# The routing's sigmoid from ScalarE's own table instead of silu times a reciprocal, in a macaron block of two mixture-of-experts layers around attention

## The chip, the cores and the metric

One core of one Trainium2 chip. The time is device microseconds of one execution; three executions of the kernel before are given below, and one more that was profiled.

## What is computed

A block of three residual steps on x of 2048 rows of 128 numbers, in fp32: half a mixture-of-experts layer, attention, half a mixture-of-experts layer with the same weights. The part that the change touches is the routing in the two expert layers (64 experts, 8 chosen):

```
aff = xf @ centroids.T
biased = aff + expert_biases
_, idx = jax.lax.top_k(biased, TOP_K)
sel = jnp.take_along_axis(aff, idx, axis=1)
w = jax.nn.sigmoid(sel)
w = w / (jnp.sum(w, axis=-1, keepdims=True) + 1e-08)
cw = jnp.zeros((T, E)).at[jnp.arange(T)[:, None], idx].add(w)
h = jax.nn.silu(jnp.einsum('td,edf->etf', xf, W_up))
y = jnp.einsum('etf,efd->etd', h, W_down)
routed = jnp.einsum('etd,te->td', y, cw)
```

xf is the layer-normed x. The kernel computes all 64 experts for every row and multiplies by `cw`, which is zero for those not chosen.

## The kernel before

Rows are worked in chunks of 512, four in each expert layer: n = 0 to 3 in the first, 4 to 7 in the second, with attention between them. A chunk has 33 units: unit 0 is the shared expert, units 1 to 32 are pairs of experts. Products are made of three fp32r matmuls each, from a high part (a copy to fp32r) and a low part (the rest) of both factors. The order on each engine is written out by hand, by unit; engines are tied by semaphores.

A unit passes through: `up` on TensorE (L874 to L876, into one of four PSUM buffers of `lrow`), silu on ScalarE (L399), the gate's multiply on VectorE (L588), the fp32r copy `hi_unit` on ScalarE (L410), the low part (L249, on GpSimd in two of three units, on VectorE where u is a multiple of 3), and `down` on TensorE (L914 to L916), four units after its `up` in TensorE's list. ScalarE's order is silu(u), then hi(u-1). `up(u)` waits until the buffer of unit u-4 is free, `down(u)` for the low part of u.

The routing of chunk n+1 is made inside chunk n. On TensorE the transposes stand at unit 8, the product with the centroids at unit 11 (into the PSUM bank `mp`), the transpose of the weights at unit 24. VectorE reads the product at units 12 and 13 (`pro_aff`), takes the reciprocal at unit 14 (`pro_top` step 0), the eight largest at 15, the mask of the chosen at 17 (L660 and L662), and the sum at 20. ScalarE makes the silu of `aff` at unit 15 (`pro_sil`, L418), and GpSimd multiplies silu, reciprocal and mask at unit 18 (`weights`). Since silu(a)/a is the sigmoid, the reciprocal of `aff`, kept away from zero by TINY, gives it. For n = 0 and n = 4 there is no chunk before: n = 0 is routed at the start, n = 4 inside and at the end of attention, and VectorE does the multiplications (`first_weights`, L668 and on).

In chunks 1 to 3 the second layer norm (for attention) of the chunk before is made too: GpSimd raises the variances to the power -1/2 (L330 and L331, `rstd(1, c - 1)`) at unit 14, behind the low part of unit 14; VectorE refines that at unit 16 (L611 to L613) and writes the normed rows (L615) at units 16 and 17; TensorE transposes them (L927) at unit 20. In chunk 0 ScalarE and GpSimd also split the later pieces of the expert weights, at even units up to 14.

ScalarE has its functions in tables; the instruction ACT_TABLE_LOAD changes the one in use. Copies need no change of it.

Of the kernel before, what the change touches and what calls it, by code (L numbers as in the profile page):

```python
# [23 lines left out]
P = 128  # L24
# [15 lines left out]
LOWEST = -3.4e38  # L40
TINY = 1e-15


def macaron_kernel(nc, x_d, wup_d, wdn_d, wsup_d, wsdn_d, cent_d, bias_d, wq_d, wk_d, wv_d, gates_d, out_d):
# [21 lines left out]
    with ExitStack() as ctx:  # L66
        def sb(name, shape, dt=F32, stack=ctx):
            return stack.enter_context(nc.sbuf_tensor(name, shape, dt))

        def sem(name):  # L70
            return ctx.enter_context(nc.semaphore(name))
# [46 lines left out]
        xn_a = sb("xn_a", [P, TPC, D], F32, ffn)  # L118
        biased_a, aff_a = sb("biased_a", [P, TPC, E], F32, ffn), sb("aff_a", [P, TPC, E], F32, ffn)
        gated = sb("gated", [P, NG, CH], F32, ffn)  # L120
# [5 lines left out]
        with ExitStack() as first:  # L126
# [5 lines left out]
        xnT, xn = [xnT_a, xnT_b], [xn_a, xn_b]  # L132
        biased, aff = [biased_a, biased_b], [aff_a, aff_b]
        pT = [sb("pT_hi", [P, 2, NT, GW], F32R), sb("pT_lo", [P, 2, NT, GW], F32R)]
# [38 lines left out]
        p_st, p_rs, p_xn, p_xT, p_hi, p_lo = (sem("p_" + n) for n in ("stats", "rstd", "xn", "xT", "hi", "lo"))  # L173
        p_aff, p_affs, p_bias, p_max, p_sil, p_top, p_w, p_inv, p_cw, p_cwT, p_cwr = (
            sem("p_" + n) for n in ("aff", "aff_read", "biased", "max", "sil", "top", "w", "inv", "cw", "cwT", "cwT_read"))

# [140 lines left out]
        def _(pool):  # L317
            steps = [0]

            def link(ins):  # L320

                steps[0] += 1
                ins.then_inc(s_pool, 1)
                pool.wait_ge(s_pool, steps[0])
# [12 lines left out]
            def weights(n):  # L337

                pool.wait_ge(p_sil, n + 1)
                pool.wait_ge(p_top, n + 1)  # L340
                link(nc.gpsimd.tensor_tensor(rec[:, :, :], rec[:, :, :], sil[:, :, :], ALU.mult))
                nc.gpsimd.tensor_tensor(rec[:, :, :], rec[:, :, :], rest[:, :, :], ALU.mult).then_inc(p_w, 1)

# [45 lines left out]
        def _(act):  # L389
# [26 lines left out]
            def pro_sil(n):  # L416
                act.wait_ge(p_affs, n + 1)
                nc.scalar.activation(sil[:, :, :], aff[n // NCH][:, :, :], ACT.Silu).then_inc(p_sil, 1)  # L418

# [54 lines left out]
            for f in range(2):  # L474
                for c in range(NCH):
# [14 lines left out]
                    for u in range(UNITS):  # L490
# [74 lines left out]
        def _(dve):  # L565
            steps = [0]

            def link(ins):

                steps[0] += 1  # L570
                ins.then_inc(s_dve, 1)
                dve.wait_ge(s_dve, steps[0])
# [60 lines left out]

            def pro_aff(n, step):

                f = n // NCH
                ps = mp[:, 0:TPC * E].rearrange("p (t e) -> p t e", e=E)
                if step == 0:
                    dve.wait_ge(p_aff, n + 1)
                    link(nc.vector.tensor_scalar(rec[:, :, :], ps, 0.0, 2 * TINY, ALU.is_ge, ALU.mult))  # L640
                    nc.vector.scalar_tensor_tensor(out=aff[f][:, :, :], in0=ps, scalar=TINY, in1=rec[:, :, :],
                                                   op0=ALU.subtract, op1=ALU.add).then_inc(p_affs, 1)
                else:
                    nc.vector.tensor_tensor(biased[f][:, :, :], ps, bc(bias[:, :]), ALU.add).then_inc(p_bias, 1)

            def pro_top(n, step):

                b = biased[n // NCH]
                if step == 0:
                    dve.wait_ge(p_affs, n + 1)  # L650
                    nc.vector.reciprocal(rec[:, :, :], aff[n // NCH][:, :, :])
                if step == 1:
# [11 lines left out]
            def first_weights(n):  # L664

                dve.wait_ge(p_sil, n + 1)
                dve.wait_ge(p_top, n + 1)
                link(nc.vector.tensor_tensor(rec[:, :, :], rec[:, :, :], sil[:, :, :], ALU.mult))  # L668
                nc.vector.tensor_tensor(rec[:, :, :], rec[:, :, :], rest[:, :, :], ALU.mult).then_inc(p_w, 1)
                pro_sum(n)  # L670
# [54 lines left out]
            for f in range(2):  # L725
                for c in range(NCH):
                    n = f * NCH + c
                    if c == 0:
                        if f == 0:
# [6 lines left out]
                            pro_lo(n)  # L736
                            pro_aff(n, 0)
                            pro_aff(n, 1)
                            for step in range(3):
                                pro_top(n, step)  # L740
                            first_weights(n)
                    for u in range(UNITS):
# [5 lines left out]
                        if c + 1 < NCH:  # L748
# [55 lines left out]
                if f == 0:  # L804
# [28 lines left out]
                    for t in range(NT):  # L833
# [20 lines left out]
                        if t == T_AFF:  # L854
                            pro_aff(NCH, 0)
                            pro_aff(NCH, 1)
                        if t > T_AFF:
                            pro_top(NCH, t - T_AFF - 1)
                    for j in range(KB):
# [287 lines left out]
```

## Time and profile before

| | us |
|---|---|
| three runs | 581.55, 583.32, 583.37 |
| median | 583.32 |
| profiled execution | 583.93 |
| its span | 582.1 |

In the profile, PE is TensorE's matmuls, PEld its weight loads, DVE VectorE, ACT ScalarE, POOL GpSimd and SP SyncE. L418 is line 418 of the kernel printed above. A matmul's own duration overlaps with its neighbours, so the starts are what to read on TensorE. On the other engines too, neighbours overlap by up to about 0.1 us.

### The profile page before, as it was taken

The numbers are of one execution on the slowest core, as the hardware profiler recorded it, in microseconds if no ns is written. First come the engines' busy times: TensorE is split into PE (matmuls) and PEld (weight loads), VectorE is DVE, ScalarE is ACT, GpSimd is POOL, SyncE is SP. The second block draws the span as 40 slices with busy tenths as digits, with TensorE's granted clock in tenths as the row PEclk, the third lists the DMA queues.
The fourth block names the chain that finished last, engine by engine and source line by source line (L and its number), as shares of the span: only waits on it lengthen the run. The fifth ranks groups of instructions, "written<-read, shape, count | busy, mean of one in ns | idle before, by whom it ended". The sixth has DMA issues, their size and how long they took to land.

```text
span 582.1 us, 8666 instructions
## 1 busy us (share of the span) xinstructions
PE 546.1 (94%) x2715; PEld 441.7 (76%) x2715; DVE 437.9 (75%) x913; ACT 406.2 (70%) x800; POOL 280.7 (48%) x248
## 2 busy tenths in 40 slices
PE   3489999899989999989999999899999999999996
PEld 2368777687867777669999999768777777877884
DVE  3778769977996686577777988788768968875663
ACT  4558776686768777476666666677776787687774
POOL 4478765666576567300000000055664766566563
PEclk9689999999999999999999999999999999999999
DMA  6465564455536645000000000046664555666562
GB/s 187 135 199 179 172 193 144 131 176 181 161 125 188 178 155 162 1 1 1 2 0 2 1 2 1 1 139 185 182 193 152 161 198 142 178 175 196 180 191 82
DMA packets 47837, 73.25 MB, mean 126 GB/s; under 512 B 8944, under 2 KB 13488, under 8 KB 47792
## 3 DMA queue, kind: packets, MB, share of 16 engines
q1 hardware_dynamic: 47792, 72.71, 41.0%
q8 instruction: 21, 0.34, 0.2%
q14 instruction: 24, 0.20, 0.1%
HBM read 70.58 MB, written 2.10 MB: 125 GB/s over the span
## 4 chain that ended last, share of the span: by engine, by line
PE 76%; DVE 12%; ACT 3%; POOL 3%; issue 3%; DMA 2%; SPq 1%; POOLq 0%; DVEq 0%; ACTq 0%
PE lrow L874 11%; PE lrow L875 11%; PE lrow L876 11%; PE bank L914 9%; PE bank L916 8%; PE bank L915 8%; PE bank L920 6%; PE bank L1069 3%; PE bank L1071 3%; PE bank L1070 3%; DVE rs L613 2%; DVE gated L588 2%; POOL gpart_lo L249 2%; DVE rs L611 1%; PE bank L875 1%
## 5 line engine op out<-in xcount | busy, mean ns | idle before, releaser
L249 POOL TENSOR_TENSOR gpart_lo<-gated,gpart_hi 128x512 fp32r<-128x512 f32 x176 | 226.6, 1293 | 192.5 <-ACT gpart_hi L410 188.4
L399 ACT ACTIVATE lrow<-lrow 128x512 f32<-128x512 f32 (+1 forms) x256 | 149.7, 585 | 62.0 <-PE lrow L876 61.7
L588 DVE TENSOR_TENSOR gated<-lrow,wide 128x512 f32<-128x512 f32 x170 | 116.5, 685 | 48.4 <-ACT lrow L399 43.7
L410 ACT CAST gpart_hi<-gated 128x512 fp32r<-128x512 f32 x176 | 107.9, 613 | 8.0 <-DVE gated L588 7.3
L914 PE MATMUL bank<-gpart_lo,wdn_hi 128*128 128x512 f32 x256 | 102.2, 399 | 1.6 <-POOL gpart_lo L249 1.4
L916 PE MATMUL bank<-gpart_hi,wdn_hi 128*128 128x512 f32 x256 | 101.6, 397 | 0.0
L915 PE MATMUL bank<-gpart_hi,wdn_lo 128*128 128x512 f32 x256 | 101.1, 395 | 0.0
L588 DVE TENSOR_TENSOR lrow<-lrow,wide 128x512 f32<-128x512 f32 x78 | 54.0, 693 | 30.8 <-ACT lrow L399 30.8
L410 ACT CAST gpart_hi<-lrow 128x512 fp32r<-128x512 f32 (+1 forms) x88 | 52.0, 591 | 30.8 <-DVE lrow L588 30.7
L810 DVE TENSOR_TENSOR pT_lo<-bank,pT_hi 128x512 fp32r<-128x512 f32 x64 | 43.6, 683 | 25.8 <-ACT pT_hi L532 25.8
L249 DVE TENSOR_TENSOR gpart_lo<-lrow,gpart_hi 128x512 fp32r<-128x512 f32 (+1 forms) x88 | 59.9, 680 | 1.3 <-ACT gpart_hi L410 0.6
L914 PEld LDWEIGHTS bank<-gpart_lo,wdn_hi 128*128 128x128 f32 x256 | 48.2, 188 | 16.0 <-POOL gpart_lo L249 4.2
L916 PEld LDWEIGHTS bank<-gpart_hi,wdn_hi 128*128 128x128 f32 x256 | 48.2, 188 | 11.8
L525 ACT ACTIVATE prow<-lrow,nmax 128x512 f32<-128x512 f32 x64 | 44.4, 696 | 17.8 <-DVE nmax L719 17.8
L915 PEld LDWEIGHTS bank<-gpart_hi,wdn_lo 128*128 128x128 f32 x256 | 48.2, 188 | 11.1
L532 ACT CAST pT_hi<-bank 128x512 fp32r<-128x512 f32 x64 | 38.0, 593 | 25.2 <-PE bank L920 25.0
L874 PE MATMUL lrow<-xnT_lo_a,wup_hi 128*128 128x512 f32 x128 | 53.5, 418 | 0.4 <-DVE gpart_lo L249 0.4
L874 PE MATMUL lrow<-xnT_lo_b,wup_hi 128*128 128x512 f32 x128 | 52.0, 406 | 0.0
L875 PE MATMUL lrow<-xnT_hi_a,wup_lo 128*128 128x512 f32 x128 | 51.7, 404 | 0.0
L876 PE MATMUL lrow<-xnT_hi_a,wup_hi 128*128 128x512 f32 x128 | 51.7, 404 | 0.0
L875 PE MATMUL lrow<-xnT_hi_b,wup_lo 128*128 128x512 f32 x128 | 50.7, 396 | 0.0
L876 PE MATMUL lrow<-xnT_hi_b,wup_hi 128*128 128x512 f32 x128 | 50.2, 392 | 0.0
(181 smaller groups left out, 989.6 us busy)
## 6 DMA issues: line engine op xcount, KB each, us to landing
wide<-gates_dram SPq DMA_DIRECT2D x496, 128.0 KB, 3.0
raw<-in_w_up SPq DMA_DIRECT2D x8, 256.0 KB, 3.9
raw<-in_w_down SPq DMA_DIRECT2D x8, 256.0 KB, 4.2
x<-in_x SPq DMA_DIRECT2D x4, 256.0 KB, 4.3
gates_dram<-gates SPq DMA_DIRECT2D x8, 128.0 KB, 2.3
out_dram<-x SPq DMA_DIRECT2D x4, 256.0 KB, 3.2
raws<-in_wv SPq DMA_DIRECT2D x1, 64.0 KB, 2.2
raws<-in_wq SPq DMA_DIRECT2D x1, 64.0 KB, 2.1
```

The costliest lines, as they stand in the source:

```text
L249: return eng.tensor_tensor(gpart[1][0:m, U % NGP, :], gated_at(U)[0:m, :], gpart[0][0:m, U % NGP, :].bitcast(F32), ALU.subtract)
L399: nc.scalar.activation(dst[0:m, :], hid[U % NH][0:m, :], ACT.Silu).then_inc(s_silu, 1)
L410: nc.scalar.copy(gpart[0][0:m, U % NGP, :], gated_at(U)[0:m, :]).then_inc(s_ghi, 1)
L525: nc.scalar.activation(prow[:, j * CH:(j + 1) * CH], lrow[:, j * CH:(j + 1) * CH], ACT.Exp, bias=nmax[:, t % 2:t % 2 + 1], accum_out=psums ...
L588: nc.vector.tensor_tensor(gated_at(U), a, b, ALU.mult).then_inc(s_gated, 1)
L810: nc.vector.tensor_tensor(pT[1][at], tb[q % 2][:, :].rearrange("p (k n) -> p k n", n=P), pT[0][at].bitcast(F32), ALU.subtract).then_inc(a_ ...
L874: nc.tensor.matmul(out, a[0], b[1], start=True, stop=False)
L875: nc.tensor.matmul(out, a[1], b[0], start=False, stop=False)
L876: return nc.tensor.matmul(out, a[0], b[0], start=False, stop=True)
L914: nc.tensor.matmul(y, w[0], g[1], start=(u == 0), stop=False)
L915: nc.tensor.matmul(y, w[1], g[0], start=False, stop=False)
L916: nc.tensor.matmul(y, w[0], g[0], start=False, stop=(u == UNITS - 1)).then_inc(s_down, 1)
```

## The change

ScalarE computes the sigmoid directly, from PSUM, at unit 13; the silu of the units uses another table, so there is one load before the sigmoid and one before the next silu. VectorE's comparison, shift and reciprocal go, and one of the two multiplications of `weights` and `first_weights`. The read of the product and the biased scores stand together at unit 12. For n = 4, whose bank is needed by attention, VectorE copies the product to `aff_b` and the sigmoid reads that, at the place that `pro_sil` had.

```diff
-                link(nc.gpsimd.tensor_tensor(rec[:, :, :], rec[:, :, :], sil[:, :, :], ALU.mult))
-                nc.gpsimd.tensor_tensor(rec[:, :, :], rec[:, :, :], rest[:, :, :], ALU.mult).then_inc(p_w, 1)
+                nc.gpsimd.tensor_tensor(rec[:, :, :], sil[:, :, :], rest[:, :, :], ALU.mult).then_inc(p_w, 1)
...
             def pro_sil(n):
-                act.wait_ge(p_affs, n + 1)
-                nc.scalar.activation(sil[:, :, :], aff[n // NCH][:, :, :], ACT.Silu).then_inc(p_sil, 1)
+                act.wait_ge(p_bias, n + 1)
+                src = flat(aff_b) if n == NCH else mp[:, 0:TPC * E]
+                nc.scalar.activation(flat(sil), src, ACT.Sigmoid).then_inc(p_sil, 1)
...
-                            if u == 15:
+                            if u == 13:
                                 pro_sil(n + 1)
...
-            def pro_aff(n, step):
+            def pro_aff(n):
 
                 f = n // NCH
                 ps = mp[:, 0:TPC * E].rearrange("p (t e) -> p t e", e=E)
-                if step == 0:
-                    dve.wait_ge(p_aff, n + 1)
-                    link(nc.vector.tensor_scalar(rec[:, :, :], ps, 0.0, 2 * TINY, ALU.is_ge, ALU.mult))
-                    nc.vector.scalar_tensor_tensor(out=aff[f][:, :, :], in0=ps, scalar=TINY, in1=rec[:, :, :],
-                                                   op0=ALU.subtract, op1=ALU.add).then_inc(p_affs, 1)
-                else:
-                    nc.vector.tensor_tensor(biased[f][:, :, :], ps, bc(bias[:, :]), ALU.add).then_inc(p_bias, 1)
+                dve.wait_ge(p_aff, n + 1)
+                if n == NCH:
+                    nc.vector.tensor_copy(aff_b[:, :, :], ps)
+                nc.vector.tensor_tensor(biased[f][:, :, :], ps, bc(bias[:, :]), ALU.add).then_inc(p_bias, 1)
...
-                if step == 0:
-                    dve.wait_ge(p_affs, n + 1)
-                    nc.vector.reciprocal(rec[:, :, :], aff[n // NCH][:, :, :])
...
-                link(nc.vector.tensor_tensor(rec[:, :, :], rec[:, :, :], sil[:, :, :], ALU.mult))
-                nc.vector.tensor_tensor(rec[:, :, :], rec[:, :, :], rest[:, :, :], ALU.mult).then_inc(p_w, 1)
+                nc.vector.tensor_tensor(rec[:, :, :], sil[:, :, :], rest[:, :, :], ALU.mult).then_inc(p_w, 1)
...
                             if u == 12:
-                                pro_aff(n + 1, 0)
-                            if u == 13:
-                                pro_aff(n + 1, 1)
-                            if u == 14:
-                                pro_top(n + 1, 0)
+                                pro_aff(n + 1)
```

## Rows read from the trace of the kernel before

**Rows 1.** The page: span, TensorE's line, the chain that ended last by engine.
```profile
span 582.1 us, 8666 instructions
...
PE 546.1 (94%) x2715; PEld 441.7 (76%) x2715; DVE 437.9 (75%) x913; ACT 406.2 (70%) x800; POOL 280.7 (48%) x248
...
PE 76%; DVE 12%; ACT 3%; POOL 3%; issue 3%; DMA 2%; SPq 1%; POOLq 0%; DVEq 0%; ACTq 0%
```

**Rows 2.** Windows: n = 5; length, busy of each engine, clock, DMA.
```profile
428.00:478.00 50.00, 49.51 (x223) 39.17 (x223) 40.31 (x80) 37.65 (x70) 31.58 (x27) 1.00 0.54 171
```

**Rows 3.** Groups by line, whole span; busy us, mean ns, idle before.
```profile
L651 DVE RECIPROCAL rec<-aff_a 128x256 f32<-128x256 f32 x4 | 7.0, 1741 | 0.0
...
L640 DVE TENSOR_SCALAR rec<-bank 128x256 f32<-128x256 f32 x8 | 3.3, 414 | 2.9 <-PE bank L876 2.9
...
L418 ACT ACT_TABLE_LOAD x2 | 2.6, 1283 | 0.0
...
L641 DVE SCALAR_TENSOR_TENSOR aff_a<-bank,rec 128x256 f32<-128x256 f32 x4 | 1.7, 424 | 0.1
...
L418 ACT ACTIVATE sil<-aff_a 128x256 f32<-128x256 f32 x4 | 1.7, 418 | 0.0
```

**Rows 4.** Timeline of ScalarE at the start; start us, us, what.
```profile
16.39 0.62 ACT L462 CAST wdn_hi<-raw 128x512 fp32r<-128x512 f32 x1 [1.81 <-DMA raw<-in_w_down]
17.02 1.28 ACT L418 ACT_TABLE_LOAD   x1
18.32 0.42 ACT L418 ACTIVATE sil<-aff_a 128x256 f32<-128x256 f32 x1
```

**Rows 5.** Timeline, all engines, n = 5, units 12 to 17.
```profile
448.94 0.60 ACT L410 CAST gpart_hi<-lrow 128x512 fp32r<-128x512 f32 x1
...
449.84 0.58 ACT L399 ACTIVATE lrow<-lrow 128x512 f32<-128x512 f32 x1 [0.31 <-PE lrow L876]
...
450.34 0.61 ACT L410 CAST gpart_hi<-gated 128x512 fp32r<-128x512 f32 x1
...
451.03 2.69 POOL L249 TENSOR_TENSOR gpart_lo<-gated,gpart_hi 128x512 fp32r<-128x512 f32 x2 [1.50 <-ACT gpart_hi L410]
...
452.85 0.67 DVE L588 TENSOR_TENSOR lrow<-lrow,wide 128x512 f32<-128x512 f32 x1
...
453.83 0.40 PE L914 MATMUL bank<-gpart_lo,wdn_hi 128*128 128x512 f32 x1
```

**Rows 6.** Timeline, all engines, n = 0, units 13 to 17.
```profile
51.07 0.59 ACT L410 CAST gpart_hi<-lrow 128x512 fp32r<-128x512 f32 x1
...
51.83 0.58 ACT L399 ACTIVATE lrow<-lrow 128x512 f32<-128x512 f32 x1 [0.17 <-PE lrow L876]
...
53.53 2.56 POOL L249 TENSOR_TENSOR gpart_lo<-gated,gpart_hi 128x512 fp32r<-128x512 f32 x2 [0.24 <-ACT gpart_hi L410]
...
55.83 0.40 PE L914 MATMUL bank<-gpart_lo,wdn_hi 128*128 128x512 f32 x1
```

**Rows 7.** Timeline, all engines, n = 1, units 15 to 20.
```profile
104.76 1.30 POOL L249 TENSOR_TENSOR gpart_lo<-gated,gpart_hi 128x512 fp32r<-128x512 f32 x1
...
106.34 1.04 POOL L331 TENSOR_TENSOR rs<-rs,mhalf 128x4 f32<-128x4 f32 x1
...
107.47 0.15 DVE L611 TENSOR_TENSOR rs<-rs 128x4 f32<-128x4 f32 x1
...
112.82 0.33 PE L927 MATMUL bank<-ident,xn 128*128 128x128 f32 x1 [1.36 <-DVE xn L615]
```

**Rows 8.** Timeline, all engines, the weights of n = 0 on VectorE.
```profile
19.32 1.45 POOL L335 TENSOR_TENSOR wup_lo<-raw,wup_hi 128x512 fp32r<-128x512 f32 x1 [0.97 <-ACT wup_hi L462]
...
20.14 0.66 DVE L680 TENSOR_SCALAR wsum<-wsum 128x4 f32<-128x4 f32 x1
```

**Rows 9.** Timeline of ScalarE, the start of n = 4.
```profile
375.97 0.37 ACT L539 CAST oT_hi<-bank 128x256 fp32r<-128x256 f32 x1 [3.33 <-PE bank L876]
...
378.89 0.59 ACT L423 CAST cwT<-bank 128x512 fp32r<-128x512 f32 x1 [0.98 <-PE bank L920]
```

More of the change, by code:

```diff
@@ L40 @@
 LOWEST = -3.4e38
-TINY = 1e-15
 def macaron_kernel(nc, x_d, wup_d, wdn_d, wsup_d, wsdn_d, cent_d, bias_d, wq_d, wk_d, wv_d, gates_d, out_d):
@@ L118, in macaron_kernel @@
         xn_a = sb("xn_a", [P, TPC, D], F32, ffn)
-        biased_a, aff_a = sb("biased_a", [P, TPC, E], F32, ffn), sb("aff_a", [P, TPC, E], F32, ffn)
+        biased_a, _ = sb("biased_a", [P, TPC, E], F32, ffn), sb("free_a", [P, TPC, E], F32, ffn)
         gated = sb("gated", [P, NG, CH], F32, ffn)
@@ L132, in macaron_kernel @@
         xnT, xn = [xnT_a, xnT_b], [xn_a, xn_b]
-        biased, aff = [biased_a, biased_b], [aff_a, aff_b]
+        biased = [biased_a, biased_b]
         pT = [sb("pT_hi", [P, 2, NT, GW], F32R), sb("pT_lo", [P, 2, NT, GW], F32R)]
@@ L173, in macaron_kernel @@
         p_st, p_rs, p_xn, p_xT, p_hi, p_lo = (sem("p_" + n) for n in ("stats", "rstd", "xn", "xT", "hi", "lo"))
-        p_aff, p_affs, p_bias, p_max, p_sil, p_top, p_w, p_inv, p_cw, p_cwT, p_cwr = (
-            sem("p_" + n) for n in ("aff", "aff_read", "biased", "max", "sil", "top", "w", "inv", "cw", "cwT", "cwT_read"))
+        p_aff, p_bias, p_max, p_sil, p_top, p_w, p_inv, p_cw, p_cwT, p_cwr = (
+            sem("p_" + n) for n in ("aff", "biased", "max", "sil", "top", "w", "inv", "cw", "cwT", "cwT_read"))
         e_y, e_yT, e_x, e_st, e_rs, e_xn, e_xT, e_hi, e_lo = (
@@ L736, in _ @@
                             pro_lo(n)
-                            pro_aff(n, 0)
-                            pro_aff(n, 1)
-                            for step in range(3):
+                            pro_aff(n)
+                            for step in range(1, 3):
                                 pro_top(n, step)
@@ L854, in _ @@
                         if t == T_AFF:
[L855 to L858, printed above, removed]
+                            pro_aff(NCH)
+                        if t == T_AFF + 2:
+                            pro_top(NCH, 1)
                     for j in range(KB):
```

## The prediction

> **What bounds the kernel now.** I read the page first: TensorE is busy for 94% of the span and carries 76% of the chain that ended last; VectorE carries 12% of it, ScalarE only 3% [rows 1]. The reader should see a kernel whose length is that of TensorE's list plus the gaps in it. The table of windows shows how few gaps there are: in the sixth chunk (n = 5) TensorE is busy 49.51 us of 50.00, at the full granted clock [rows 2]. So what delays a TensorE matmul there is paid in full, and nothing is given back later. The question of this change is therefore how late the other engines may be before a `down` matmul waits for them.
>
> The timeline of n = 5 gives that margin [rows 5]. The fp32r copy of unit 13 (`hi_unit`) starts on ScalarE at 450.34; GpSimd then makes the low parts of units 13 and 14, a pair that starts at 451.03 and takes 2.69 us, so the first, at the 1.30 us of one [rows 7], is done at 452.33; `down(13)` starts on TensorE at 453.83. The margin is 1.50 us. ScalarE has little to catch up with: in this stretch it idles 0.31 us a unit [rows 5], waiting for TensorE. In n = 0 the weight pieces are split by ScalarE in the same loop and margins are smaller: low part 13 starts at 53.53, is done 1.28 us (half of the pair's 2.56) later at 54.81, and `down(13)` starts at 55.83, a margin of 1.02 us [rows 6].
>
> **The change, part by part.**
>
> *Removed from VectorE*, eight times: the comparison (0.41 us), the shift by TINY (0.42 us) and the reciprocal (1.74 us), 2.57 us of instructions [rows 3] and about 2.45 us of its queue, since neighbours overlap a little. GpSimd and, for n = 0 and 4, VectorE lose one 128x256 multiply. For n = 4 a copy of 0.41 us (priced as the comparison, which has its shape) comes in for the two removed ones, beside attention, where nothing waits for it: 0.
>
> *Added to ScalarE*: two table loads for each sigmoid, one ahead of it, one ahead of the next silu. All loads in the trace take 1283 ns [rows 3]. What surrounds one is seen at n = 0: the copy ends at 17.01, the load runs from 17.02 to 18.30, the activation starts at 18.32 [rows 4]. A switch costs the queue 1.30 us. The sigmoid itself reads PSUM instead of SBUF; I price it as the silu, 0.42 us [rows 3].
>
> The Trainium skill (ScalarE: Activation LUTs, section "What ACT_TABLE_LOAD costs") gives 2.66 us a switch, 1.28 of load and 1.38 of drain; rows 4 agree with the first figure and show no drain. With its figure the sum below would be 6 x 2 x 1.36 = 16 us larger, an estimate from that page. I take the row.
>
> *Moved*: `pro_sil` goes from unit 15 to unit 13 on ScalarE, behind `hi_unit(12)`. Behind it in the queue stand silu(14), hi(13), silu(15), hi(14) and so on: everything on which `down(13)` and later ones depend. It now waits for `p_bias`, which VectorE gives after gate(12), before hi(12) is over; no further wait.
>
> *The burst.* 2 x 1.30 + 0.42 = 3.02 us lies between hi(12) and silu(14). In n = 5 hi(12) ends at 448.94 + 0.60 = 449.54, so silu(14) starts at 452.56, where it started at 449.84: 2.72 us late [rows 5]. hi(13) is late by the same 2.72, low part 13 too, and `down(13)` by 2.72 - 1.50, 1.2 us, and the start after a wait: 1.3 us.
>
> *Does VectorE's relief repay this?* Before, gate(15) started at 452.85, late because of the reciprocal [rows 5]. Now hi(13) follows silu(14) by 0.50 (as before) and silu(15) follows that by 0.50: 453.56; it takes 0.58, and gate(15) starts at 454.17, 1.32 us later than before. VectorE idles through the burst; its 2.45 us saved are spent waiting for ScalarE. From gate(15) on its list (maximum, gates, match) is full and everything keeps this lateness. So both routes give 1.3 us, and n = 4, 5 and 6, whose chunks have the same spacing, cost 3 x 1.3 = **3.9 us**.
>
> *n = 0.* hi(12) ends at 51.66; silu(14) goes from 51.83 to 54.68, 2.85 late; `down(13)` is late by 2.85 - 1.02, with the start after a wait **1.9 us** [rows 6].
>
> *n = 1 and 2.* The same burst, and a third party. In these chunks GpSimd's queue has, behind low part 14, the power for the second layer norm (`rstd(1, ..)`), on which VectorE's L611 waits at unit 16. Before, low part 14 ended at 106.06, the power at 107.38, and L611 started at 107.47, just as VectorE came free [rows 7]: no margin. Now low parts 13 and 14 start 2.7 us late, but run without the gap between them, 2.56 instead of 2.69 us [rows 5, 6], so the power ends 2.55 us late. L611, the normalised rows and the transposes at unit 20, where TensorE already waited for VectorE in this chunk (1.36 us before one of them) [rows 7], are all 2.5 us late. VectorE alone would be 1.3 late; GpSimd's queue doubles it. 2 x 2.5 = **5.0 us**. Should L611 now also collide with low part 16, as L613 may do anyway, 1.3 us are added in each; that is the upper bound, 2.6 more.
>
> *n = 3 and 7* have no routing for a next chunk: 0. *Start of the first half:* the sigmoid waits for a weight piece and a load as the silu did. One 128x256 multiply fewer is on VectorE's way (0.42 us, as L641 of that shape), but L680 (4 numbers a partition) took 0.66 us and ended when GpSimd's instruction from 19.32 to 20.77 did [rows 8]. Started that much earlier it would end at the same 20.8. I take 0, with -0.5 as the bound; the second load falls in ScalarE's wait for the gate weights. The Trainium skill (SBUF — State Buffer, on the shared port pair) says that the loser of the two engines blocks for a whole instruction. This row agrees: by that page 0, without it -0.5.
>
> *Start of the second half (n = 4):* one load replaces the silu's, one is new, at about 376.34, after the last copy of attention's output. It ends at 377.62; the two silus behind it, at a pitch of 0.5, end by 378.7, before the copy to `cwT` behind them, which waited until 378.89 for TensorE [rows 9]. Hidden: 0; if that cover were gone, 1.3 us.
>
> *Sum:* 1.9 + 5.0 + 3.9 = 10.8 us. The profiled execution took 583.93 us (582.1 of span, 1.8 around it); 583.93 + 10.8 = 594.7. It stands 0.6 above the median of 583.32, so against that: **594.1 us**, 1.9% slower.
>
> **The rivals.**
>
> *A. GpSimd's queue does not double the cost in n = 1 and 2.* If the power gets done in time, they cost 1.3 each by TensorE's and VectorE's routes: 594.1 - 2.4 = 591.7. For it: before, VectorE stood in no wait there. Against: low part 14 is ahead of the power in one queue, and must itself follow the burst. 0.12.
>
> *B. Faster: the burst is not seen.* If the two functions share a table, or the loads are slipped into ScalarE's idle moments, ScalarE's queue is as long as before, and VectorE's 2.45 us a chunk count: TensorE's waits for normalised rows in n = 1 and 2 (1.36 us at one of them, and a smaller one) vanish, some 1.9 a chunk, and the start gives up to 0.5: 583.3 - 3.8 - 0.5 = 579.0. It decides if the burst stays below about 1.5 us, the margin of rows 5. Against: no row shows a load beside another ScalarE instruction, and a chunk offers 0.3 us of idle at a time. The case that the change does not do what it says (no loads) is this one. 0.06.
>
> *C. A switch costs much more inside a full queue than in rows 4.* With margins used up all of it passes: at twice the row, 6 x 2 x 1.3 = 15.6 more, 609.7. The trace's loads stand behind copies or after waits, never in the middle of silus; but the one of rows 4 had a full queue on both sides. The Trainium skill's figure, named above, is on this side. 0.04.
>
> *D. Nothing to measure.* The margins would have to be twice as large; the slacks of rows 5 and 6 exclude it, unless gains of B and losses cancel. 0.03.
>
> **How the numbers follow.** The forecast has 0.75, A 0.12, B 0.06, C 0.04, D 0.03. The prediction is 594.1. The bounds: from below A, -0.5 at the start and about 1 for small margins misread over six chunks, 590; from above 2.6 for the collision and 1.3 for the second half's start, 598. The range is 589.5 to 598.5; it holds the forecast and A. Differences of 0.3% are about what a measurement of this kernel tells from none. Slower 0.91, same 0.03, faster 0.06.
>
> **What would show it.** In the changed profile: 1283 ns loads, 16 for the sigmoids and their returns, with the three others; silu(14) some 3.0 us after the end of hi(12) in every routing chunk; VectorE idle there, before gate(14), with ScalarE as releaser; a new wait of TensorE on GpSimd's low part at `down(13)` of about 1.2 us; L611 waiting about 1 us for L331's result in n = 1 and 2 alone; chunk lengths up by 1.9, 2.5, 2.5, 0, 1.3, 1.3, 1.3, 0. The prediction is wrong if the loads overlap with other ScalarE work, if a chunk after the burst wins back part of it (a gap of TensorE elsewhere that closes), or if low part 14 does not hold up the power.

## The result, and the profile after

| | before | after |
|---|---|---|
| median, us | 582.62 (4 runs, 581.55 to 583.37) | 595.01 (4 runs, 593.92 to 597.45) |
| profiled execution, us | 583.93 | 595.85 |
| its span, us | 582.1 | 594.0 |

The changed kernel takes 1.0194 times as long (95% interval 1.0168 to 1.022). The medians differ by 12.4 us, and their quotient, 1.021, lies inside the interval too. The two profiled executions differ by 11.92 us, and that is the difference taken apart below.

Line numbers of the changed kernel: silu L397, `hi_unit` L408, the sigmoid L417, the gate L587, low part L248, `up` L860 to L862, `down` L900 to L902, the power L330, its refinement L610 to L612, the normed rows L614, their transposes L913, mask L653 and L655.

The page after, which answers to [rows 1]: span, engines, and the chain that ended last.

```profile
span 594.0 us, 8649 instructions
...
PE 549.5 (92%) x2715; PEld 443.8 (75%) x2715; DVE 416.6 (70%) x888; ACT 423.9 (71%) x814; POOL 276.6 (47%) x242
...
PE 71%; DVE 10%; ACT 6%; POOL 5%; issue 4%; DMA 2%; SPq 1%; POOLq 0%; DVEq 0%; ACTq 0%
```

VectorE has 21 us less to do and the kernel is 12 us longer. ScalarE has 18 us more: 20.6 us of loads for the sigmoids, where 2.6 stood before. In the chain that ended last, ScalarE's share has doubled from 3 to 6% and GpSimd's has risen from 3 to 5%. The groups by line say which instructions (busy us, mean ns, idle before):

```profile
L900 PE MATMUL bank<-gpart_lo,wdn_hi 128*128 128x512 f32 x256 | 103.5, 404 | 8.6 <-POOL gpart_lo L248 8.4
...
L417 ACT ACT_TABLE_LOAD x8 | 10.3, 1283 | 0.1
L397 ACT ACT_TABLE_LOAD x8 | 10.3, 1283 | 0.1
...
L469 ACT ACT_TABLE_LOAD x1 | 1.3, 1283 | 0.7 <-PEq L1126 0.7
L436 ACT ACT_TABLE_LOAD x1 | 1.3, 1283 | 0.0
L439 ACT ACT_TABLE_LOAD x1 | 1.3, 1283 | 0.0
```

Sixteen loads and three others, all of 1283 ns. TensorE's matmuls on a low part (L900) had 8.4 us of waits for GpSimd ahead of them.

How late the changed kernel is at a point, against the trace of before, can be read off TensorE's first `up` of each chunk. The same rows of the two kernels, first before (chunks 5 and 6), then after:

```profile
425.95 0.39 PE L874 MATMUL lrow<-xnT_lo_b,small_hi 128*64 128x512 f32 x1
...
476.08 0.40 PE L874 MATMUL lrow<-xnT_lo_b,small_hi 128*64 128x512 f32 x1
```

```profile
435.61 0.39 PE L860 MATMUL lrow<-xnT_lo_b,small_hi 128*64 128x512 f32 x1
...
486.88 0.39 PE L860 MATMUL lrow<-xnT_lo_b,small_hi 128*64 128x512 f32 x1
```

Chunk 5 took 50.13 us and takes 51.27: 1.14 more. The whole table, made in this way, in us; everything up to `up(11)` of n = 0 is counted as the start:

| | start | n=0 | n=1 | n=2 | n=3 | n=4 | n=5 | n=6 | n=7 | sum |
|---|---|---|---|---|---|---|---|---|---|---|
| predicted | 0 | 1.9 | 2.5 | 2.5 | 0 | 1.3 | 1.3 | 1.3 | 0 | 10.8 |
| measured | -0.54 | 1.76 | 4.66 | 2.54 | 0.01 | 1.23 | 1.14 | 1.12 | 0.01 | 11.93 |

Within a chunk the lateness comes in steps. In n = 4, 5 and 6 the only large step up is at unit 18 of TensorE's list (1.32, 1.31 and 1.32), just ahead of which `down(13)` stands; 0.17 to 0.18 is given back at units 22 and 23. The same is given back there in experiment 1, so it belongs to VectorE's shorter list.

### The profile page after: what moved, and what is told of

Read it like the earlier page. It is cut to its first block, busy times and chain, and to the rows that moved or that the text cites. A ratio compares the mean times of both kernels' runs of the same rounds, so it can differ in the third digit from the quotient of the medians.

```text
span 594.0 us, 8649 instructions
## 1 busy us (share of the span) xinstructions
PE 549.5 (92%) x2715; PEld 443.8 (75%) x2715; DVE 416.6 (70%) x888; ACT 423.9 (71%) x814; POOL 276.6 (47%) x242
## 4 chain that ended last, share of the span: by engine, by line
PE 71%; DVE 10%; ACT 6%; POOL 5%; issue 4%; DMA 2%; SPq 1%; POOLq 0%; DVEq 0%; ACTq 0%
PE lrow L860 11%; PE lrow L861 10%; PE lrow L862 10%; PE bank L900 8%; PE bank L902 8%; PE bank L901 7%; PE bank L906 5%; POOL gpart_lo L248 3%; PE bank L1055 3%; PE bank L1057 3%; PE bank L1056 3%; ACT gpart_hi L408 2%; DVE rs L610 2%; DVE rs L612 1%; ACT lrow L397 1%
## 5 line engine op out<-in xcount | busy, mean ns | idle before, releaser
L248 POOL TENSOR_TENSOR gpart_lo<-gated,gpart_hi 128x512 fp32r<-128x512 f32 x176 | 227.2, 1296 | 211.4 <-ACT gpart_hi L408 207.3
L397 ACT ACTIVATE lrow<-lrow 128x512 f32<-128x512 f32 (+1 forms) x256 | 149.6, 584 | 66.4 <-PE lrow L862 65.4
L587 DVE TENSOR_TENSOR gated<-lrow,wide 128x512 f32<-128x512 f32 x170 | 117.0, 688 | 71.3 <-ACT lrow L397 64.5
L408 ACT CAST gpart_hi<-gated 128x512 fp32r<-128x512 f32 x176 | 107.8, 613 | 10.2 <-DVE gated L587 9.8
L900 PE MATMUL bank<-gpart_lo,wdn_hi 128*128 128x512 f32 x256 | 103.5, 404 | 8.6 <-POOL gpart_lo L248 8.4
L902 PE MATMUL bank<-gpart_hi,wdn_hi 128*128 128x512 f32 x256 | 102.1, 399 | 0.0
L587 DVE TENSOR_TENSOR lrow<-lrow,wide 128x512 f32<-128x512 f32 x78 | 54.3, 696 | 35.7 <-ACT lrow L397 35.7
L408 ACT CAST gpart_hi<-lrow 128x512 fp32r<-128x512 f32 (+1 forms) x88 | 52.0, 591 | 22.3 <-DVE lrow L587 22.1
L900 PEld LDWEIGHTS bank<-gpart_lo,wdn_hi 128*128 128x128 f32 x256 | 48.6, 190 | 25.4 <-POOL gpart_lo L248 11.6
L248 DVE TENSOR_TENSOR gpart_lo<-lrow,gpart_hi 128x512 fp32r<-128x512 f32 (+1 forms) x88 | 60.0, 682 | 1.1 <-ACT gpart_hi L408 0.6
L902 PEld LDWEIGHTS bank<-gpart_hi,wdn_hi 128*128 128x128 f32 x256 | 48.6, 190 | 12.0
L860 PE MATMUL lrow<-xnT_lo_a,wup_hi 128*128 128x512 f32 x128 | 53.9, 421 | 0.2 <-DVE gpart_lo L248 0.2
L862 PE MATMUL lrow<-xnT_hi_a,wup_hi 128*128 128x512 f32 x128 | 52.1, 407 | 0.0
L860 PE MATMUL lrow<-xnT_lo_b,wup_hi 128*128 128x512 f32 x128 | 51.7, 404 | 0.0
L862 PE MATMUL lrow<-xnT_hi_b,wup_hi 128*128 128x512 f32 x128 | 50.2, 392 | 0.0
```

The source lines that it names most:

```text
L248: return eng.tensor_tensor(gpart[1][0:m, U % NGP, :], gated_at(U)[0:m, :], gpart[0][0:m, U % NGP, :].bitcast(F32), ALU.subtract)
L397: nc.scalar.activation(dst[0:m, :], hid[U % NH][0:m, :], ACT.Silu).then_inc(s_silu, 1)
L408: nc.scalar.copy(gpart[0][0:m, U % NGP, :], gated_at(U)[0:m, :]).then_inc(s_ghi, 1)
L587: nc.vector.tensor_tensor(gated_at(U), a, b, ALU.mult).then_inc(s_gated, 1)
L860: nc.tensor.matmul(out, a[0], b[1], start=True, stop=False)
L862: return nc.tensor.matmul(out, a[0], b[0], start=False, stop=True)
```

## The burst, read in n = 5

The burst is the load, the sigmoid and the load back, one behind the other in ScalarE's queue. The timeline of the changed kernel (start us, us, what, idle before and who ended it); it answers to [rows 5].

```profile
458.60 0.59 ACT L408 CAST gpart_hi<-lrow 128x512 fp32r<-128x512 f32 x1
...
459.21 1.28 ACT L417 ACT_TABLE_LOAD   x1
...
460.51 0.38 ACT L417 ACTIVATE sil<-bank 128x256 f32<-128x256 f32 x1
...
460.91 1.28 ACT L397 ACT_TABLE_LOAD   x1
...
462.20 0.58 ACT L397 ACTIVATE lrow<-lrow 128x512 f32<-128x512 f32 x1
...
462.82 0.69 DVE L587 TENSOR_TENSOR gated<-lrow,wide 128x512 f32<-128x512 f32 x1 [2.81 <-ACT lrow L397]
...
463.39 2.51 POOL L248 TENSOR_TENSOR gpart_lo<-gated,gpart_hi 128x512 fp32r<-128x512 f32 x2 [4.20 <-ACT gpart_hi L408]
...
464.70 0.49 PE L900 MATMUL bank<-gpart_lo,wdn_hi 128*128 128x512 f32 x1 [1.05 <-POOL gpart_lo L248]
```

The copy ends at 459.19 and the next silu starts at 462.20: 3.01 us for two loads and a sigmoid, nothing else between them. VectorE idles 2.81 us ahead of gate(14) and GpSimd 4.20 us ahead of its pair; the first low part of the pair is done at 464.65 (half of 2.51 after 463.39), and `down(13)` starts at 464.70 after a wait.

## n = 1: where the miss is

```profile
107.33 2.52 POOL L248 TENSOR_TENSOR gpart_lo<-gated,gpart_hi 128x512 fp32r<-128x512 f32 x2 [4.21 <-ACT gpart_hi L408]
...
110.12 1.04 POOL L330 TENSOR_TENSOR rs<-rs,mhalf 128x4 f32<-128x4 f32 x1
...
111.13 1.30 POOL L248 TENSOR_TENSOR gpart_lo<-gated,gpart_hi 128x512 fp32r<-128x512 f32 x1
111.19 1.25 DVE L610 TENSOR_TENSOR rs<-rs 128x4 f32<-128x4 f32 x1 [1.03 <-POOL rs L330]
...
116.27 1.03 DVE L614 TENSOR_SCALAR xn<-x,mv,rs 128x128 f32<-128x128 f32 x2
...
116.66 0.47 PE L913 MATMUL bank<-ident,xn 128*128 128x128 f32 x1 [2.63 <-DVE xn L614]
```

These rows answer to [rows 7]. The power follows the two low parts and is done at 111.16; VectorE waited 1.03 us for it and then needed 1.25 us for four numbers a partition (it took 0.15 before), while GpSimd's low part runs beside it. The transposes wait 2.63 us, 1.27 more than before: with the step of 1.30 at unit 18 that is 2.6. The long L610 is no addition: before, GpSimd's low part of unit 16 lay beside the last of the three instructions of the refinement, and that one took 1.15 us; now it takes 0.16. Rows of before, then of after:

```profile
107.68 1.29 POOL L249 TENSOR_TENSOR gpart_lo<-gated,gpart_hi 128x512 fp32r<-128x512 f32 x1 [0.31 <-ACT gpart_hi L410]
...
107.85 1.15 DVE L613 SCALAR_TENSOR_TENSOR rs<-rs 128x4 f32<-128x4 f32 x1
```

```profile
112.68 0.16 DVE L612 SCALAR_TENSOR_TENSOR rs<-rs 128x4 f32<-128x4 f32 x1
```

In n = 2 it is the same to the hundredth (a wait of 2.63 at 175.14), and that chunk costs 2.54.

Only n = 1 has a further 1.9 us (steps of 0.84 and 1.06 at units 22 and 23). The windows around it (from and to; length; busy of PE, PEld, DVE, ACT, POOL; granted clock; DMA), before and after:

```profile
116.00:120.00 4.00, 4.00 (x20) 3.15 (x19) 3.93 (x9) 3.34 (x8) 3.19 (x4) 1.00 0.59 186
```

```profile
112.00:116.00 4.00, 2.03 (x10) 1.40 (x8) 3.86 (x15) 1.10 (x2) 1.62 (x2) 1.00 0.18 66
116.00:120.00 4.00, 3.12 (x8) 2.35 (x9) 3.94 (x8) 2.06 (x5) 3.08 (x5) 0.51 0.19 69
120.00:124.00 4.00, 4.00 (x12) 3.11 (x12) 3.54 (x7) 2.39 (x6) 2.71 (x3) 0.63 0.61 210
...
176.00:180.00 4.00, 3.77 (x17) 2.75 (x17) 3.87 (x8) 3.58 (x7) 3.65 (x4) 1.00 0.38 113
```

TensorE is busy from 120 to 124 and has 12 matmuls in those 4 us, where the kernel before has 21: its granted clock is at the lower level (0.5, 1.2 GHz) from 116.12 to 122.94. It had been busy 2.03 of the 4 us ahead of 116. In n = 2 there is the same wait, and TensorE was busy for only 1.00 of the 4 us from 172 to 176, yet the clock stayed full (last row).

## The experiments

Each was timed beside the kernel before on the same chip: 1 to 4 on one chip and 5 to 8 on another (585.0 us for the kernel before on both), 9 and the repeat of 8 on a third (585.2). The row `after` is from the first comparison, where the kernel before had 582.62. So rows are compared by their ratios and not by their medians. The columns n=1 to end give how late TensorE starts the chunk, against the one trace of before, in us; they are of one profiled execution each.

| kernel | median | ratio (interval) | n=1 | n=2 | n=3 | n=4 | n=5 | n=6 | n=7 | end |
|---|---|---|---|---|---|---|---|---|---|---|
| after | 595.01 | 1.0194 (1.0168 to 1.022) | 1.22 | 5.88 | 8.42 | 8.43 | 9.66 | 10.80 | 11.92 | 11.93 |
| 1 silu twice, no loads | 583.46 | 0.9979 (0.9964 to 0.9995) | -1.83 | -1.70 | -1.65 | -1.63 | -1.92 | -2.09 | -2.28 | -2.28 |
| 2 before + loads | 599.45 | 1.0253 (1.0232 to 1.0274) | 2.05 | 5.69 | 8.03 | 8.05 | 10.52 | 12.90 | 15.24 | 15.25 |
| 3 power at 12 | 591.21 | 1.0119 (1.0077 to 1.0161) | 3.14 | 4.59 | 5.97 | 5.29 | 6.46 | 7.61 | 8.73 | 8.74 |
| 4 sigmoid at 17 | 587.21 | 1.0046 (1.0027 to 1.0064) | 1.02 | 0.58 | 0.13 | 0.16 | 1.30 | 2.47 | 3.61 | 3.62 |
| 5 sigmoid at 15 | 593.20 | 1.0144 (1.0113 to 1.0175) | 0.20 | 3.16 | 6.39 | 6.39 | 7.85 | 9.13 | 10.44 | 10.45 |
| 6 before, power at 12 | 584.29 | 0.9985 (0.9967 to 1.0003) | 0.05 | 0.07 | 1.10 | 0.42 | 0.45 | 0.47 | 0.43 | 0.44 |
| 7 tanh | 582.79 | 0.9958 (0.9942 to 0.9974) | -1.88 | -1.94 | -2.08 | -1.88 | -2.19 | -2.35 | -2.58 | -2.57 |
| 8 tanh, power at 12 | 579.86 | 0.9916 (0.9895 to 0.9937) | -1.10 | -1.88 | -2.70 | -3.37 | -3.57 | -3.73 | -3.92 | -3.91 |
| 8 again | 579.20 | 0.9901 (0.9881 to 0.9921) | -3.30 | -4.03 | -4.83 | -5.49 | -5.66 | -5.83 | -6.02 | -6.02 |
| 9 and norm earlier | 581.71 | 0.9945 (0.9926 to 0.9965) | -1.25 | -1.49 | -1.84 | -1.15 | -1.26 | -1.42 | -1.61 | -1.60 |

**1. The change without its loads.** The sigmoid's place takes a silu, whose table is the one in use; the routing weights of the output are then others, the work is the same.

```diff
-                nc.scalar.activation(flat(sil), src, ACT.Sigmoid).then_inc(p_sil, 1)
+                nc.scalar.activation(flat(sil), src, ACT.Silu).then_inc(p_sil, 1)
```

> The changed kernel with the silu function in the sigmoid's place, so that no table is changed inside a chunk; the routing weights are other numbers, everything else stands where it stood. If the two loads are the cost: the burst between hi(12) and silu(14) falls from 3.0 to 0.4 us, no down matmul waits, and the time is that of the kernel before or a little less, 580.5 to 582.5 us. I expect no gain from VectorE's saved 2.45 us a chunk in n = 1 and 2, since L610 (the refinement of the layer norm) then waits for GpSimd's power, which ends where it ended before. If instead the new place of the sigmoid, its read from PSUM or the shorter VectorE list is the cost: 590 or more. If VectorE's saved time is worth what rival B says: 579.

583.46 us, ratio 0.9979. All of the loss is the loads; what VectorE was relieved of is worth 0.2 to 0.3 us in each of n = 4 to 6 and nothing in n = 1 and 2. There VectorE comes to the refinement earlier than before and waits 0.52 us for GpSimd's power, as was expected.

**2. The loads without the change.** The kernel before, with one sigmoid of one number a partition at unit 13.

```diff
+                            if u == 13:
+                                nc.scalar.activation(eps[:, 4:5], eps[:, 0:1], ACT.Sigmoid)
```

> The kernel before, with a sigmoid of one number per partition put into ScalarE's list at unit 13 of the six routing chunks: it brings two table loads and about 0.2 us, and takes nothing off VectorE. My theory: silu(14) is 2.5 us late, and VectorE, which still has its reciprocal, stands 2.3 us later at gate(15); about 2.3 us in each of n = 0, 4, 5, 6 and 2.5 in n = 1, 2: 14 us, with a longer stretch of half clock in n = 1 up to 16, so 596 to 599. VectorE's relief in the change is then worth only some 4 us of the 15 us that it frees. If the relief were worth all it frees, the loads alone would cost 12.4 + 6 x 2.45 = 27 us: 609.

599.45 us, a ratio of 1.0253 where the whole change has 1.0194. Here VectorE still has its reciprocal, right behind the loads, and n = 4 to 6 cost 2.3 to 2.5 each:

```profile
464.08 1.75 DVE L653 RECIPROCAL rec<-aff_b 128x256 f32<-128x256 f32 x1
...
465.37 0.49 PE L916 MATMUL bank<-gpart_lo,wdn_hi 128*128 128x512 f32 x1 [0.87 <-POOL gpart_lo L249]
...
468.16 0.50 PE L876 MATMUL lrow<-xnT_lo_b,wup_hi 128*128 128x512 f32 x1 [0.43 <-DVE gpart_lo L249]
```

After `down(13)`, TensorE waits twice more, for VectorE's low parts of units 15 and 18 (0.43 us here, 0.48 at `up(22)`). So what the change takes away is worth about 1.2 us a chunk once ScalarE is late, though it was worth 0.2 in experiment 1. That the reciprocal and its two helpers are all of these 1.2 is argued: this kernel also keeps the silu of `aff` on ScalarE at unit 15 (0.42 us) and GpSimd's second multiply, and its mask (named below at experiment 4) took 1.55 us in n = 5 where the changed kernel has 0.42, while its burst is 0.2 us shorter. n = 1 costs 1.3 more than n = 2 (3.64 and 2.34); the granted clock was at the lower level from 119.20 to 122.62.

**3. GpSimd's power ahead of the late low parts.** The changed kernel with `rstd(1, c - 1)` at unit 12 on GpSimd.

```diff
-                        if f == 0 and c and u == 14:
+                        if f == 0 and c and u == 12:
```

> The changed kernel with the power of the second layer norm (rstd(1, ..)) at unit 12 of GpSimd's list, ahead of low parts 13 and 14. If GpSimd's queue doubles the cost in n = 1 and 2: L610 no longer waits for it, VectorE is 1.3 us late there instead of 2.5, and the time falls by 2.5 us; if the stretch of half clock at 116 to 123 us comes from TensorE's longer wait at unit 20, it goes too, 2 us more: 590.5 to 592.5. If VectorE's own list sets that wait: no change, 595.

591.21 us. The rows of n = 1 to set beside those above:

```profile
105.31 1.04 POOL L330 TENSOR_TENSOR rs<-rs,mhalf 128x4 f32<-128x4 f32 x1
...
109.24 2.52 POOL L248 TENSOR_TENSOR gpart_lo<-gated,gpart_hi 128x512 fp32r<-128x512 f32 x2 [2.89 <-ACT gpart_hi L408]
...
112.00 0.15 DVE L610 TENSOR_TENSOR rs<-rs 128x4 f32<-128x4 f32 x1
...
117.41 0.33 PE L913 MATMUL bank<-ident,xn 128*128 128x128 f32 x1 [1.46 <-DVE xn L614]
```

VectorE waits for nothing at L610, which takes 0.15 us, and the transposes wait 1.46 where they waited 2.63. n = 1 and 2 have one large step each, 1.31 at unit 18: the doubling was GpSimd's queue. The stretch at the lower clock in n = 1 is not in this trace, but there is one in n = 0, from 58.96 to 62.37, behind the wait for low part 13 (1.78 us; it was 1.77 in the changed kernel, where the clock stayed full); it cost 1.5. One trace each does not show that the edit removed the stretch in n = 1.

**4 and 5. The same burst at another unit.**

```diff
-                            if u == 13:
+                            if u == 17:
```

> The changed kernel with the sigmoid and its two loads at unit 17 of ScalarE's list instead of unit 13. In n = 1 and 2 ScalarE there idles 1.9 us for gate(17) before, so the burst is mostly hidden, and VectorE's mask no longer collides with low part 17: -0.9 us each. In n = 4, 5, 6 hi(17) stands behind the burst, and its margin is 1.5 as at unit 13: +1.25 each; n = 0: +1.3. With -0.5 at the start: 582.6 + 2.8, so 584 to 587. If a switch costs its full 3 us wherever it stands: 595 or more.

587.21 us. n = 4 to 6 cost 1.14 to 1.17 each, as much as with the burst at unit 13 (1.12 to 1.23). The step up, 1.26, is at unit 22 now, and `down(17)` waits for GpSimd's low part:

```profile
460.63 1.27 POOL L248 TENSOR_TENSOR gpart_lo<-gated,gpart_hi 128x512 fp32r<-128x512 f32 x1 [2.82 <-ACT gpart_hi L408]
...
461.95 0.50 PE L900 MATMUL bank<-gpart_lo,wdn_hi 128*128 128x512 f32 x1 [1.07 <-POOL gpart_lo L248]
```

But n = 1 and 2 gain 0.45 each; 0.9 was expected. The burst stands behind the power and falls into the time in which TensorE stood in its wait for the normed rows anyway, so that no further wait shows. The gain comes with VectorE's mask (L662 before), which stands ahead of the second pair of normed rows. In n = 1 and 2 of every other run it lies beside a low part of GpSimd and takes 1.46 to 1.55 us; here the burst holds GpSimd's low part of unit 17 back until 112.69, and the mask is over by then. A row of before, then of this run:

```profile
111.05 1.47 DVE L662 TENSOR_TENSOR rest<-rest,biased_a 128x256 f32<-128x256 f32 x1
```

```profile
112.13 0.43 DVE L655 TENSOR_TENSOR rest<-rest,biased_a 128x256 f32<-128x256 f32 x1
```

With `u == 15` in the same line:

> The changed kernel with the sigmoid and its loads back at unit 15, where the silu of the kernel before stood: does the move from 15 to 13 cost anything by itself? By the same reckoning the burst now lies between hi(14) and silu(16): gate(16) and low(15) are 2.0 us late on VectorE, up(19) and up(22) wait for them, in every routing chunk; GpSimd's power is in front of the burst and no longer late. n = 0, 1, 2, 4, 5, 6 cost some 2.0 each, 12, less 0.8 at the start: 11 us more than before, ratio 1.018 to 1.022, with a longer stretch of half clock up to 1.024. If the move to 13 is what costs: ratio 1.010 or less.

593.20 us, a ratio of 1.0144 where 1.018 to 1.022 was expected. n = 4 to 6 cost 1.3 to 1.5, less than the 2.0 of the expectation. The first to be late is `up(19)`, as expected: low part 15 is VectorE's, done in place in `lrow`, and `up(19)` waits for that buffer.

```profile
465.16 0.50 PE L860 MATMUL lrow<-xnT_lo_b,wup_hi 128*128 128x512 f32 x1 [1.22 <-DVE gpart_lo L248]
```

n = 1 and 2 cost 2.96 and 3.23. Of each, 1.5 is there by `up(20)`, and 0.7 is a longer wait for the normed rows (2.07 and 2.06 us, where the kernel before has 1.36 and 1.38). The rest, 0.8 and 1.0, falls in stretches at the lower clock, 3.4 us each (from 115.25 and 173.28).

**6. The power at unit 12 in the kernel before.** The edit of experiment 3.

> The kernel before with the power at unit 12 of GpSimd's list instead of 14. VectorE came to the refinement (L611) 0.09 us after the power was done, so it waited for its own list, not for GpSimd: no change, ratio 0.998 to 1.002. If GpSimd's power was already what held TensorE's transposes at unit 20: up to 3.5 us faster, 0.994.

584.29 us, ratio 0.9985, an interval that includes 1. n = 1 takes as long as before to 0.02 us: GpSimd's queue did not hold VectorE there in the kernel before. In n = 3 it did. No routing is made there, so VectorE comes early, and at 212.62 of the kernel before L611 had waited 0.59 us for the power; here it waits for nothing, and the chunk is 0.7 us shorter. One stretch at the lower clock (from 167.84) cost 1.1 in n = 2, behind a wait for the normed rows (1.37) that the kernel before has in the same place (1.38).

**7. Half of tanh instead of the sigmoid.** sigmoid(a) = (1 + tanh(a/2)) / 2, and the half cancels against the sum, with 2e-8 for 1e-8. GpSimd adds the 1 beside other work, for the chunks routed inside others; VectorE does both in one instruction for n = 0 and 4.

```diff
+                link(nc.gpsimd.tensor_scalar(rec[:, :, :], sil[:, :, :], 1.0, None, ALU.add))
...
-                nc.gpsimd.tensor_tensor(rec[:, :, :], sil[:, :, :], rest[:, :, :], ALU.mult).then_inc(p_w, 1)
+                nc.gpsimd.tensor_tensor(rec[:, :, :], rec[:, :, :], rest[:, :, :], ALU.mult).then_inc(p_w, 1)
...
-                nc.scalar.activation(flat(sil), src, ACT.Sigmoid).then_inc(p_sil, 1)
+                nc.scalar.activation(flat(sil), src, ACT.Tanh, scale=0.5).then_inc(p_sil, 1)
```

> The changed kernel with tanh(x/2) for the sigmoid: sigmoid is (1 + tanh(x/2))/2, the half cancels in the normalisation (with 2e-8 for 1e-8 beside the sum), and the 1 is added by GpSimd ahead of its multiply (in VectorE's multiply for n = 0 and 4). If tanh stands in the table that silu is taken from, the trace has 5 loads and the time is that of the run with silu in the sigmoid's place, 1 to 2.5 us below the kernel before, ratio 0.996 to 0.999. If it needs a table of its own, the time is that of the changed kernel.

582.79 us, ratio 0.9958. In this table and in experiment 1's, what lies ahead of n = 1 is mostly the start, of which more below. All loads of its trace:

```profile
L398 ACT ACT_TABLE_LOAD x2 | 2.6, 1283 | 0.0
L470 ACT ACT_TABLE_LOAD x1 | 1.3, 1283 | 0.7 <-PEq L1128 0.7
L437 ACT ACT_TABLE_LOAD x1 | 1.3, 1283 | 0.0
L440 ACT ACT_TABLE_LOAD x1 | 1.3, 1283 | 0.0
```

Five, as many as before: in the chunks, tanh stands beside silu without a load. It needs none behind the exponential of attention either: the tanh of n = 4 runs at 368.14 with no load ahead of it, and the load stands ahead of the next silu. With the loads gone the kernel runs as experiment 1 did: from the start of n = 1 on it wins 0.7, and experiment 1 won 0.45.

**8. Tanh, and the power at unit 12.**

> The same with the power at unit 12 of GpSimd's list. Now nothing stands between VectorE's saved 2.45 us and the normed rows of n = 1 and 2: TensorE's waits at unit 20 (1.9 us in each) go. 3.8 us less than the tanh kernel, ratio 0.988 to 0.992. If the saved time has no use even then, because something else is late for unit 20: as the tanh kernel.

579.86 us, ratio 0.9916. The gain in n = 1 and 2 is 0.8 each where up to 1.9 was expected, and 0.7 in n = 3, which was not expected; experiments 3 and 6, which have the same edit, have it too. As a second look:

> The version with tanh and GpSimd's power at unit 12 once more, beside the one with the norm earlier on the same chip, so that the two are compared directly. Expected: ratio to before 0.991 to 0.992, as in its first run.

579.20 us, ratio 0.9901, a little below the 0.991 to 0.992 expected. What TensorE still waits for at unit 20 in n = 1 of this run, and what VectorE did ahead of it:

```profile
103.53 0.15 DVE L611 TENSOR_TENSOR rs<-rs 128x4 f32<-128x4 f32 x1
...
104.12 1.58 DVE L615 TENSOR_SCALAR xn<-x,mv,rs 128x128 f32<-128x128 f32 x2
...
107.11 1.49 DVE L656 TENSOR_TENSOR rest<-rest,biased_a 128x256 f32<-128x256 f32 x1
108.53 0.88 DVE L615 TENSOR_SCALAR xn<-x,mv,rs 128x128 f32<-128x128 f32 x2
...
108.99 0.79 PE L915 MATMUL bank<-ident,xn 128*128 128x128 f32 x2 [0.80 <-DVE xn L615]
```

The mask (L656) takes 1.49 us here, beside a low part of GpSimd from 107.03 to 108.32; in experiment 4, clear of it, the same instruction took 0.43. The second pair of rows stands behind it.

**9. The norm two units earlier on VectorE as well.**

```diff
-                                if u == 16:
+                                if u == 14:
...
-                                if u == 17:
+                                if u == 15:
```

> The version with tanh and GpSimd's power issued at unit 12, and VectorE's n=1 norm refinement and multiply issued two units earlier, at units 14 and 15 instead of 16 and 17. Theory: what TensorE still waits for at the transposes of unit 20 in n=1 and n=2 (0.8 us each twice) is VectorE's late rows, so the wait goes: up to 1.3 us in each of the two chunks, 2.6 us below the version without this edit, ratio to before 0.985 to 0.989. Rival: the rows are late because VectorE's four numbers collide with GpSimd's low parts wherever they are put, or because the VectorE queue as a whole is the later one; then no change, ratio 0.991 to 0.992. Second rival: at units 14 and 15 the refinement waits for GpSimd's power and holds back the gate behind it; then up to 2 us slower in the two chunks.

581.71 us, ratio 0.9945, where 0.985 to 0.989 was expected: slower than experiment 8 beside it on the chip (0.9901, the intervals don't meet). The wait at unit 20 is gone (the step there is -2.17 against the kernel before), and two others have come, 0.39 us ahead of `down(19)` for a low part of GpSimd, and a larger one at `up(19)`:

```profile
102.20 1.27 DVE L611 TENSOR_TENSOR rs<-rs 128x4 f32<-128x4 f32 x1
...
103.70 1.17 DVE L613 SCALAR_TENSOR_TENSOR rs<-rs 128x4 f32<-128x4 f32 x1
...
105.42 0.69 DVE L588 TENSOR_TENSOR lrow<-lrow,wide 128x512 f32<-128x512 f32 x1
...
108.37 0.50 PE L862 MATMUL lrow<-xnT_lo_a,wup_hi 128*128 128x512 f32 x1 [1.14 <-DVE gpart_lo L248]
```

The refinement now stands beside the pair of low parts 13 and 14 on GpSimd and takes 1.27 and 1.17 us in two instructions of 0.15 to 0.17. gate(15) starts at 105.42, behind it and the first rows. In the repeat of experiment 8 it starts at 100.93, in a chunk that began 2.05 us earlier, so it is 2.4 us later now. `up(19)` waits for unit 15's buffer. This step is 1.16 to 1.30 in each of n = 1, 2 and 3. Against the repeat, n = 1 and 2 cost some 0.5 more each and n = 3 costs 1.3 more: experiment 8 wins 0.7 in it, and here it loses 0.7.

So the expectation was wrong, and neither rival was right as a whole. The first named the collision with GpSimd's low parts, which the rows show, but said that nothing would change. The second said slower, but named a wait for GpSimd's power, which the rows do not show, and did not count n = 3. Experiment 8 is the best version: 5 to 6 us faster than the kernel before.

## Why the prediction was right

594.1 us was predicted and 595.01 measured, inside the range of 589.5 to 598.5, and slower, as forecast at 0.91. The mechanism is the one that was forecast, and the terms of the chunks came out within 0.2 us but for n = 1. That the sum is as near as it is, 10.8 against 11.92, is in part luck: 1.9 us more in n = 1 and 0.5 less at the start, neither of them in the sum, partly cancel. By its steps:

- **Removed from VectorE, nothing gained.** Right for n = 1 to 6: experiment 1 has all of that relief and no loads, and wins 0.2 to 0.3 us a chunk in n = 4 to 6 and none in n = 1 and 2. The words that VectorE's 2.45 us "are spent waiting for ScalarE" say too much: by experiment 2, without the relief n = 4 to 6 would have cost some 2.4 us each, so about half of it held the cost down to the 1.3 of the sum.
- **A switch costs 1.30 us of queue.** Right: 459.21 to 460.51 and 460.91 to 462.20. The sixteen loads of the sigmoids and their returns all take 1.31 us from the end of the instruction before to the start of the next, and twelve of them stand in the middle of the silus of a chunk. Case C is excluded, and the runs decide against the 2.66 us that the Trainium skill gives (ScalarE: Activation LUTs, section "What ACT_TABLE_LOAD costs"): its 1.28 of load agrees, its 1.38 of drain does not show.
- **The burst, 3.0 us, and the margin of 1.50 us.** Right: 3.01, and a step of 1.32 against 1.3. What is given back later (0.17 to 0.18) was not in the sum, and "nothing is given back later" was wrong by that much.
- **n = 0, 1.9.** 1.76 measured from `up(11)` on: a step of 2.0 at unit 18, and the rest given back.
- **GpSimd doubles it in n = 1 and 2, 2.5 each.** Right: 2.54 in n = 2, and experiment 3 takes the power out of the late queue and leaves 1.31. Case A is excluded. Experiment 6 shows that in n = 1 and 2 this was no wait of the kernel before: the change made it. "In n = 1 and 2 alone" was wrong: in n = 3, L610 waits 0.59 us for the power in both kernels, at no added cost. The collision of L610 with low part 16, given as a possible 1.3 more in each, did happen (1.25 us), but it only took the place of that of L613 in the kernel before, so nothing was added.
- **Start, 0 with -0.5 as the bound.** -0.54 in the profiled pair, but that it lies at the bound is luck. The multiply is gone, and as predicted L672 (L680 before) still ended only when GpSimd's instruction beside it did (19.53 and 19.50), after 0.93 us. In this execution a weight piece also landed 1.05 us earlier (its copy starts at 15.34, at 16.39 in [rows 4]), and the multiply by the inverse sum started 1.27 us earlier, of which that piece is most. The rest is the clock's. The kernel before had the lower level from 20.10 to 30.34; in the changed one matmuls are at the slow pitch (0.43 us) only until 27.07, and it is 2.05 us ahead at `down(0)`. Then it has the lower level from 37.61 to 44.44 where the kernel before had it from 40.58 to 43.99, and 1.5 us are given back by `up(11)`. The start differs from run to run: of two executions of the same kernel, experiment 8 and its repeat, the one that had no stretch at the lower clock from 37.8 to 44.6 started chunk 1 2.2 us ahead of the other. No gain or loss of the start below that can be told from these traces.
- **n = 4's start, 0.** Right: n = 4 is entered as late as n = 3 was (8.42 and 8.43).
- **The burst is not seen (case B), or only noise (D).** Excluded by the sixteen loads and by experiment 1 against the change.
- **What was missing: 1.9 us of TensorE's clock in n = 1.** The text priced waits as waits alone. Behind a wait of 2.63 us the granted clock fell to its lower level for 6.8 us. The wait alone does not decide it: n = 2 of the same execution had the same wait and none of it. Two of the three other executions of the changed kernel had spans of 592.1 and 592.4 against 594.0, the third 595.6; they have no trace of their own, and their mean granted clocks (0.994, 0.985 and 0.984, against 0.988) do not single it out, so that the difference is this stretch is not shown. What decides whether the clock falls stays open.

Of the expectations of the experiments, that of experiment 9 failed, and three failed in size. Experiment 8 gained 0.8 of 1.9 us: with GpSimd's power out of the way, VectorE's second pair of rows is still late, behind a mask that takes 1.49 us beside GpSimd's low part. No run has the power at unit 12 and the mask clear of that low part, so that this is all of what is left is argued. Experiment 5 named the right consumer, `up(19)`, and took 2.0 us for a step of 1.4. Experiment 4 gained half of what was expected in n = 1 and 2.

## What to carry to other kernels

A function of ScalarE is priced by its neighbours on that engine: 0.38 us of sigmoid between silus cost 3.0 us of queue, and one from the table in use (tanh, by an identity) cost 0.4. Where an engine in mid-pipeline stalls, take the stall less the margin of the first instruction that waits for it, then follow each other queue that stands behind the late work: GpSimd's power, unrelated to the sigmoid, doubled the price in two chunks, and moving the burst behind it (unit 17) took back 8 of the 12 us (11.93 late at the end, and 3.62). An instruction is moved to where its inputs are early and its neighbours on the other engines are harmless too: two units earlier put four numbers beside a low part, and 0.15 us became 1.27.

## What the runs showed of the hardware

- A table load between two instructions costs its 1283 ns and 10 to 20 ns on each side; the sixteen of the changed kernel and those of experiments 4 and 5 agree. Silu and tanh need none between them while silu's table is in use, and tanh none behind attention's exponential (experiment 7); silu and sigmoid need one each way.
- VectorE instructions of four numbers a partition take 0.15 us alone and up to 1.27 us when GpSimd works beside them (L610, L611, L613 above): with GpSimd's low part at 102.16, L611 from 102.20 ends at 103.47, when half of that pair's 2.69 us is over.
- The mask, one VectorE instruction on 128x256 numbers with two inputs, takes 0.43 us clear of GpSimd (experiment 4, n = 1) and 1.46 to 1.55 us beside one of its low parts (n = 1 and 2 of the other runs).
- TensorE's granted clock fell to the lower level for 3.4 or 6.8 us behind waits in some places and executions and not in others. Where it fell in mid-kernel it cost 0.8 and 1.0 (experiment 5), 1.1 (experiment 6, n = 2), 1.3 (experiment 2, n = 1), 1.5 (experiment 3, n = 0) and 1.9 us (after, n = 1). Where two kernels differ by 0.3%, 1.7 us here, one such stretch is as large as the difference, so the clock has to be looked up in the windows before a step of one chunk is explained.
